# Splitting the expert weight loads in three, moving the fetch of the sorted rows to GpSimd, and reordering the quad loop of a routed feed-forward layer

## The reference

```
x = hidden_states.reshape(-1, h)
shared_out = _swiglu(x, shared_gate_w, shared_up_w, shared_down_w)
logits = x @ gate_w
topk_ids = jnp.argmax(logits, axis=-1)
topk_val = jnp.max(logits, axis=-1)
scores = jax.nn.sigmoid(topk_val)[:, None]
xs = x * scores
order = jnp.argsort(topk_ids)
sorted_x = xs[order]
g = _grouped_mm(sorted_x, routed_gate_w, tokens_per_expert)
u = _grouped_mm(sorted_x, routed_up_w, tokens_per_expert)
d = _grouped_mm(jax.nn.silu(g) * u, routed_down_w, tokens_per_expert)
routed_out = d[inv]
return (shared_out + routed_out).reshape(b, s, h)
```

## Time and profile before

| what | us |
|---|---|
| median of 3 runs (353.39 to 355.84) | 354.5 |
| the profiled execution's own time | 352.22 |
| its span | 350.4 |
| TensorE busy | 300.3 |
| VectorE busy | 206.3 |
| ScalarE busy | 134.8 |
| GpSimd busy | 56.0 |
| transfers issued by SyncE, share of 16 DMA engines | 47.9% |
| mean granted clock of TensorE | 0.951 |

### The profile page before, as it was taken

One profiled execution on the slowest core, in us unless ns is written; L12 is line 12 of the kernel. 1 busy time (PEld: TensorE's weight loads), 2 busy tenths in 40 slices (PEclk: granted clock), 3 DMA queues, 4 the chain that ended last, 5 costly groups with the idle time before them and its releaser, 6 DMA issues.

```text
span 350.4 us, 6874 instructions
## 1 busy us (share of the span) xinstructions
PE 300.3 (86%) x2484; PEld 213.8 (61%) x2484; DVE 206.3 (59%) x589; ACT 134.8 (38%) x309; POOL 56.0 (16%) x73
## 2 busy tenths in 40 slices
PE   1996979388899999999975999989899999964958
PEld 1774548277899999998963766665454555421322
DVE  0454684433465665665266699948739867645653
ACT  1021242243242242242233466529147545615650
POOL 0111000100110110110000001111711210442350
PEclk9999899879999999999997799999999999996996
DMA  7999991003364264053597200000389996899231
GB/s 291 397 435 426 410 316 48 2 0 111 131 241 151 91 239 147 34 181 129 233 353 285 85 2 2 6 4 0 86 299 395 394 354 251 336 358 397 49 46 17
DMA packets 13115, 67.73 MB, mean 193 GB/s; under 512 B 1738, under 2 KB 7322, under 8 KB 8986
## 3 DMA queue, kind: packets, MB, share of 16 engines
q1 hardware_dynamic: 11050, 64.28, 47.9%
q0 software_dynamic: 2032, 3.02, 4.1%
HBM read 61.38 MB, written 5.91 MB: 192 GB/s over the span
## 4 chain that ended last, share of the span: by engine, by line
PE 64%; issue 11%; DMA 10%; DVE 8%; ACT 3%; SPq 1%; DVEq 1%; POOL 1%; ACTq 0%
PE P L340 17%; PE P L460 8%; PE P L448 8%; PE P L628 7%; DMA arena<-experts_dram 7%; PE P L374 4%; PE P L484 4%; PE P L510 3%; PE P L436 2%; PE P L641 2%; DMA vrow<-sorted_x 2%; DMA arena<-patches_dram 2%; PE P L525 1%; DVE arena L996 1%; PE P L535 1%
## 5 line engine op out<-in xcount | busy, mean ns | idle before, releaser
L340 PE MATMUL P<-arena 128*104 128x256 f32 x288 | 73.5, 395 | 9.4 <-DMA arena<-patches_dram 7.1
L340 PEld LDWEIGHTS P<-arena 128*104 128x104 f32 x288 | 47.4, 176 | 22.4 <-issue 8.3
L1290 POOL TENSOR_TENSOR rstd<-var,mhalf 104x1 f32<-104x1 f32 x40 | 21.9, 548 | 210.5 <-DVE var L919 210.5
L628 PE MATMUL P<-arena,cols 128*32 128x512 f32 x288 | 37.3, 664 | 11.1 <-ACT cols L849 9.1
L824 ACT ACTIVATE arena<-arena 128x1024 f32 x31 | 31.5, 1051 | 21.2 <-SPq L325 9.1
L460 PE MATMUL P<-arena 128*128 128x104 f32 x256 | 29.9, 275 | 2.4 <-ACT arena L764 2.4
L460 PEld LDWEIGHTS P<-arena 128*128 128x128 f32 x256 | 29.7, 192 | 3.1 <-issue 1.4
L448 PEld LDWEIGHTS P<-arena 128*128 128x128 f32 x256 | 29.8, 192 | 1.2 <-issue 0.7
L448 PE MATMUL P<-arena 128*128 128x104 f32 x256 | 29.8, 275 | 0.5 <-issue 0.5
L628 PEld LDWEIGHTS P<-arena,cols 128*32 128x32 f32 x288 | 9.1, 120 | 32.6 <-issue 19.1
L764 ACT ACTIVATE arena<-P,arena 128x104 f32<-128x104 f32 x64 | 17.0, 348 | 27.7 <-PE P L448 27.7
(11 more groups left out here) (200 smaller groups left out, 480.3 us busy)
## 6 DMA issues: line engine op xcount, KB each, us to landing
arena<-experts_dram SPq DMA_DIRECT2D x22, 1536.0 KB, 8.4
arena<-experts_dram SPq DMA_DIRECT2D x8, 2048.0 KB, 12.7
arena<-patches_dram SPq DMA_DIRECT2D x4, 624.0 KB, 6.3
sorted_x<-arena SPq DMA_DIRECT2D x1, 2056.0 KB, 35.2
arena<-shared_dram SPq DMA_DIRECT2D x1, 1536.0 KB, 32.4
arena<-w_dram SPq DMA_DIRECT2D x1, 1024.0 KB, 9.8
out_dram<-arena SPq DMA_DIRECT2D x1, 1024.0 KB, 33.7
out_dram<-h POOLq DMA_DIRECT2D x8, 104.0 KB, 4.9
```

What stands on the lines that cost most here:

```text
L340: last = mm(P[b][0:a.shape[1], col:col + D], a, rhs(c), start=(c == 0), stop=(c == chunks - 1))
L628: last = mm(P[b][part, :], xT[:, c, part], weights(u)[:, c * INNER:(c + 1) * INNER], start=(c == 0), stop=(c == DC - 1), tile_position=(0, ...
L1290: nc.gpsimd.tensor_tensor(rstd[:, :], var[:, :], mhalf[:, :], ALU.pow).then_inc(s["rstd_ready"], 1)
```

## The change

- A weight load becomes three transfers of a third (gate, up, down) on the same semaphore; it counts as landed when all three have.
- GpSimd issues the three fetches of quads 0 to 6 right after its scatter; SyncE issues weights alone.
- `x3T` lies in the place of the queries, `zB` in that of the padded keys. The first copies wait for the scaled rows and no longer for `hid_ready`; `hidden(5)`, `(6)` and `(7)` come between and behind the copies of quad 0, and `hidden(3)` behind the first table.
- On TensorE the products that turn the tables round stand one `shared_up` piece earlier each. `shared_down(1)` moves ahead of quad 0; the others are spread as none, 2, 3, 4 and 5, 6 and 7 over quads 0 to 4 (before: 1; 2 and 3; 4 and 5; 6 and 7 over quads 0 to 3).
- `y_evac` writes into the rows of its own quad, so nothing waits for an earlier addition; target rows are computed for eight quads at once.
- In the loop the rows of the coming quad are fetched one turn ahead and transposed first, and ScalarE and VectorE copy gate and up weights before `hT_evac` and `y_evac`. Two fetches, of blocks 8 and 9, take the place of one, and `sorted_x` is one block longer.
- The register loads drop their bounds checks (one assertion is left where five or more stood).

```diff
-SORTED = (MAX_QUADS + 1) * 128
+BLOCKS = MAX_QUADS + 2
+SORTED = BLOCKS * 128
-YBUFS = 4
+SHARED_FIRST = 2
+SHARED_AT = ((), (2,), (3,), (4, 5), (6, 7), (), (), ())
-        oT = x3T = kz
+        oT = kz
+        x3T = qT
-        zB = flat5[:, 0:2 * HALF].rearrange("p (a n) -> p a n", a=2)
+        zB = quad[:, 0:2 * HALF].rearrange("p (a n) -> p a n", a=2)
             def feed(of, lane):
                 e, at, free = of
                 sp.wait_ge(s["copied_dve"], free)
                 sp.wait_ge(s["copied_act"], free)
-                sp.dma_start(feeds_s[:, bass.ds(at, SLOT)], experts1[bass.ds(e, 1)].rearrange("e p n -> (e p) n")).then_inc(lane_in[lane], 16)
+                for n in range(3):
+                    sp.dma_start(feeds_s[:, bass.ds(at + n * THIRD, THIRD)],
+                                 experts1[bass.ds(e, 1), :, n * THIRD:(n + 1) * THIRD].rearrange("e p n -> (e p) n")).then_inc(lane_in[lane], 16)
             feed(entry(0), 0)
             second = entry(1)
-            sp.wait_ge(xs_sent, 16 * GROUPS)
-            window(0)
             feed(second, 1)
-            for i in range(1, len(WINDOW_PARTS)):
-                window(i)
             with pe.Fori(0, more) as i:
+                pe.wait_ge(l_window_in, 16 * (i + 2))
+                xt(STILL).then_inc(s["l_xt_done"], 1)
                 pe.wait_ge(s["l_hT_ready"], i + 1)
 ...
                 down_strips(STILL % 2).then_inc(s["l_dn_done"], 1)
-                pe.wait_ge(l_window_in, 16 * (i + 2))
-                xt(STILL).then_inc(s["l_xt_done"], 1)
             with act.Fori(0, more) as i:
-                act.wait_ge(s["l_ht_done"], i + 1)
-                hT_evac().then_inc(s["l_hT_ready"], 1)
                 need, where = weights_of(act, i + (STILL + 1))
                 act.wait_ge(s["loaded"], need)
                 copy_third(where[2], 0, gate_of(2))
                 copy_third(where[3], 0, gate_of(3))
+                act.wait_ge(s["l_ht_done"], i + 1)
+                hT_evac().then_inc(s["l_hT_ready"], 1)
+                act.wait_ge(s["l_xt_done"], i + 2)
+                xT_evac().then_inc(s["l_xT_ready"], 1)
                 copy_third(where[2], 1, up_of(2)).then_inc(s["l_gatew_in"], 1)
             dve.wait_ge(s["table_ready"], 1)
             need, where = weights_of(dve, 0)
-            hidden(7)
-            dve.wait_ge(s["hid_ready"], 2 * IC)
             dve.wait_ge(s["loaded"], need)
+            dve.wait_ge(s["xs_scaled"], GROUPS)
             copy_gate(where).then_inc(s["gatew_in"], 1)
+            hidden(5)
             copy_up(where).then_inc(s["upw_in"], 1)
-            shared_rows(0)
+            hidden(6)
             copy_down(where, 0).then_inc(s["copied_dve"], 1)
             need, where = weights_of(dve, 1)
+            hidden(7)
             with dve.Fori(0, more) as i:
 ...
+                mul().then_inc(s["l_hw_ready"], 1)
+                dve.wait_ge(l_window_in, 16 * (i + 2))
                 ids = xw[:, STILL, D:XROW]
 ...
                 dve.wait_ge(s["l_aimed"], i + 1)
+                dve.wait_ge(s["l_added"], 16 * (i + 2))
             pool.wait_ge(xs_sent, 16 * GROUPS)
+            for i, q in enumerate(WINDOW_PARTS):
+                end = (WINDOW_PARTS + (STILL,))[i + 1]
+                pool.dma_start(xw[:, q:end, :], sorted_x[q * 128:end * 128, :].rearrange("(r p) c -> p r c", p=128)).then_inc(windows_in[i], 16)
+                if r == STILL - 1:
+                    pool.wait_ge(s["l_xt_done"], 1)
+                    window(STILL + 1)
             with pool.Fori(0, more) as i:
-                pool.wait_ge(s["l_aim_ready"], i + 1)
-                pool.wait_ge(s["l_xt_done"], i + 1)
                 pool.wait_ge(s["l_turn"], i + 1)
-                window(i + (STILL + 1))
                 pool.wait_ge(s["l_y_ready"], i + 2)
 ...
                 add_rows(STILL, s["l_added"])
+                pool.wait_ge(s["l_xt_done"], i + 2)
+                pool.wait_ge(s["l_aim_ready"], i + 1)
+                window(i + (STILL + 2))
```

More of the change, by code:

```diff
@@ L44 @@
 SPILLS = STILL + 1
-YBUFS = 4
+SHARED_FIRST = 2
+SHARED_AT = ((), (2,), (3,), (4, 5), (6, 7), (), (), ())
 ROUND = float(2 ** 23)
 XROW = D + 1
+IN_TABLE = "VectorE bounds each entry when it makes the table"
 BQ0, BK0, LNS, LNB, AB, BQ1, BK1, B2, B1 = 0, 2, 4, 6, 8, 10, 12, 14, 30
@@ L195, in tower @@
         l_window_in = sem("l_window_in")
-        added = [sem(f"added{r}") for r in range(STILL)]
+        added = sem("added")
         pat_in = [sem(f"pat_in{i}") for i in range(4)]
@@ L298, in entry @@
                 row = table[0:1, FEED * n:FEED * (n + 1)] if isinstance(n, int) else table[0:1, bass.ds(n * FEED, FEED)]
-                _, (e, at, free) = nc.values_load_multi_w_load_instructions(row, engines=[sp.engine], min_val=0, max_val=(SLOTS - 1) * SLOT)
-                e = nc.s_assert_within(e, 0, EXPERTS - 1, skip_runtime_bounds_check_because="the table clamps it to EXPERTS - 1")
-                return e, at, nc.s_assert_within(free, 1, MAX_QUADS + 1, skip_runtime_bounds_check_because="the table keeps it at 1 or above")
+                _, (e, at, free) = nc.values_load_multi_w_load_instructions(row, engines=[sp.engine], min_val=0, max_val=(SLOTS - 1) * SLOT,
+                                                                              skip_runtime_bounds_check_because=IN_TABLE)
+                e = nc.s_assert_within(e, 0, EXPERTS - 1, skip_runtime_bounds_check_because=IN_TABLE)
+                return e, at, nc.s_assert_within(free, 1, MAX_QUADS + 1)
             def feed(of, lane):
@@ L601, in _ @@
             last.then_inc(s["prefix_done"], 1)
-            for n in range(2, 5):
+            for n in range(2, 4):
                 shared_up(n)
@@ L608, in _ @@
             last.then_inc(s["feeds_done"], 1)
-            shared_up(5)
+            shared_up(4)
             pe.wait_ge(s["blocks_ready"], 1)
@@ L613, in _ @@
             mm(records[:, :, LANES], tcol[0:64, 1:2], ident[0:64, bass.ds(LANES - 1, 16, LANES)], start=True, stop=True).then_inc(s["table_done"], 1)
-            for n in range(6, 2 * IC):
+            for n in range(5, 2 * IC):
                 shared_up(n)
@@ L651, in shared_down @@
                 rows(6 + g % 2, lambda c: hidT[:, c, gcol(g)], lambda c: sdw[:, c, :], IC).then_inc(s["sd_done"], 1)
-            shared_down(0)
+            for g in range(SHARED_FIRST):
+                shared_down(g)
             pe.wait_ge(s["table_ready"], 1)
@@ L681, in _ @@
                     next_xt(q + 1)
-                if q == 0:
-                    shared_down(1)
-                elif q <= 3:
-                    shared_down(2 * q)
-                    shared_down(2 * q + 1)
+                for g in SHARED_AT[q]:
+                    shared_down(g)
                 if q >= 1:
@@ L1243, in _ @@
                     aim_static()
[L1244 to L1247 removed]
+                for g in SHARED_AT[q]:
+                    shared_rows(g)
                 if q >= 1:
                     dve.wait_ge(s["dn_done"], q)
[L1250 to L1252 removed]
+                    y_evac(xw[:, q - 1, 0:D]).then_inc(s["y_ready"], 1)
                 if q < STILL:
@@ L1260, in _ @@
             nc.vector.nop().then_inc(s["l_turn"], 1)
-            dve.wait_ge(added[STILL - YBUFS], 16)
             with dve.Fori(0, more) as i:
-                dve.wait_ge(s["l_added"], 16 * (i + 1))
-                dve.wait_ge(l_window_in, 16 * (i + 1))
+                need, where = weights_of(dve, i + (STILL + 1))
+                dve.wait_ge(s["loaded"], need)
+                copy_gate(where)
+                copy_up(where).then_inc(s["l_gatew_in"], 1)
+                dve.wait_ge(s["l_dn_done"], i + 1)
+                y_evac(y_last).then_inc(s["l_y_ready"], 1)
+                copy_down(where, STILL % 2).then_inc(s["copied_dve"], 1)
+                dve.wait_ge(s["l_sgate_ready"], i + 1)
+                dve.wait_ge(s["l_up_done"], i + 1)
+                mul().then_inc(s["l_hw_ready"], 1)
+                dve.wait_ge(l_window_in, 16 * (i + 2))
                 ids = xw[:, STILL, D:XROW]
@@ L1334, in _ @@
                 add_rows(STILL, s["l_added"])
-            for r in range(STILL):
-                pool.wait_ge(added[r], 16)
-            pool.wait_ge(l_window_in, 16 * (more + 1))
+                pool.wait_ge(s["l_xt_done"], i + 2)
+                pool.wait_ge(s["l_aim_ready"], i + 1)
+                window(i + (STILL + 2))
+            pool.wait_ge(added, 16 * STILL)
+            pool.wait_ge(l_window_in, 16 * (more + 2))
             pool.wait_ge(s["l_added"], 16 * (more + 1))
```

66 lines of the change are left out of this document (24 added, 42 removed).

## The result

The change makes the kernel slower: 362.14 us (356.02 to 366.25, 20 runs) against 354.71 us (352.06 to 356.12, 20 runs) for the kernel before on the same chip, +7.4 us in the medians. The ratio of undisturbed runs is 1.0123, 95% interval 1.0097 to 1.0150; that comparison leaves out runs over 1.5% above a kernel's fastest, and the changed kernel's own runs spread over 10 us, so its ratio lies under that of the medians, 1.021. The prediction was 355.1, in a range of 351.3 to 359.0: wrong.

A forecast was written before the change was run, and what follows sets the result against it. Bound: a chain of waits, the moment quad 4 is copied, five loads at full rate, then the end. Terms 0 - 1.4 + 0.8 + 1.2 = +0.6 us on 354.5 gave 355.1 us, range 351.3 to 359.0.

The forecast's parts named there:

- A: From the last shared_up piece's start to the tenth load's issue, which follows quad 4's copies; predicted -1.4 us.
- B: From the tenth load's issue to the last load's landing, the last five loads; predicted +0.8 us.
- the thirds: Weight loads split in three: shorter rows cost the last five loads 0 to 1.5 us; taken as +0.8.
- C: From the last load's landing to the end of quad 7's ht; the prediction had no term for it.
- the end: From the end of quad 7's ht to the span's end: later eviction, a last fetch behind the product; +1.2 us.
- its own signs: Wrong if five loads took under 23 or over 28 us, quad 4 was copied before 298 or after 302, or clock stayed full.
- the barrier behind the last landing: At the program's end, a barrier after a later landing; 0.2 us within the +1.2.
- quad 4: Copied earlier because TensorE's pieces are spread differently, so the load of 301.44 is issued at 300.0; -1.4 us.
- Earlier start of the loads: 0: First two loads begin some 3.3 us earlier, but later loads wait for slots; worth 0, at most 3.3 us.
- My rival for GpSimd's fetches: GpSimd's five fetches go out late beside VectorE's copies of quad 0, quad 1 slips 3 us: 358.1 us; chance 0.07.
- each third pays a start of its own: Each added transfer of the last five loads costs 0.5 us, thirds cost 5.0: 359.3 us; chance 0.15.
- Stage D: From the end of quad 7's ht to the span's end, 15.4 us before; predicted +1.2 us.

The follow-up runs named there:

- e6: The changed kernel with the three fetches of quads 0 to 6 back on SyncE and the second load behind the scatter; +7.1 us, ratio 1.012 to the kernel before.
- e11: e8 with ScalarE's gate and up copies again ahead of the last quad's eviction; +0.5 us, ratio 0.999 to the kernel before.
- e15: e8 repeated unchanged on another occasion; -0.3 us, ratio 0.989 to the kernel before.
- e16: e8 with VectorE's y_evac moved ahead of the up weights' copies in the loop; -0.6 us, ratio 0.994 to the kernel before.
- e1: The changed kernel run again as a control; +8.9 us, ratio 1.022 to the kernel before.
- e8: e4 plus the three fetches on SyncE and the second load behind the scatter; 350.9 us, -3.1 us, ratio 0.990 to the kernel before.
- e4: The changed kernel with whole loads, the last fetch early and hT_evac ahead of the loop's copies; 357.9 us, +3.1 us, ratio 1.008 to the kernel before.
- e14: The kernel before with only the weight loads split into thirds; +2.4 us, ratio 1.006 to the kernel before.
- e9: e8 with the weight loads in thirds again; +1.2 us, ratio 0.999 to the kernel before.
- e2: The changed kernel with the loop's last fetch released ahead of the blank quad's product; +5.8 us, ratio 1.013 to the kernel before.
- e10: e8 with the last fetch again waiting for target rows behind the blank quad's product; -0.6 us, ratio 0.998 to the kernel before.
- e5: The kernel before, unchanged, one profile as a control; no timing given, 43.3 us from the last shared_up piece's start to the tenth load's issue.
- e12: The kernel before with only the three fetches moved to GpSimd, second load not waiting for the scatter; +0.2 us, ratio 0.998 to the kernel before.
- e13: e4 with GpSimd still fetching but the second load held until the scatter has landed; +2.6 us, ratio 1.010 to the kernel before.
- e7: The changed kernel with GpSimd still fetching but the second load held until the scatter has landed; +8.6 us, ratio 1.025 to the kernel before.

## Why the prediction was wrong

The sum gave +0.6 us, the profiled executions +7.4. By stages, measured less predicted: A -1.1 (-2.5 against -1.4), B +3.1 (+3.9 against the thirds' +0.8), C +1.7 (not in the sum), the end +3.1 (+4.3 against +1.2). By its own signs, too, it was wrong: the last five loads took 29 us, over its 28. The steps that failed are the thirds, stage C, and the barrier behind the last landing; the head start cost something in other executions.

- **What bounds the kernel, and quad 4: right, a little too careful.** Quads 0, 1 and 3 start at 265.1, 270.9 and 287.2, predicted 266.0, 271.7 and 287.9; the tenth load is issued at 299.0, not 300.0. Stage A is 2.5 us shorter, the term was -1.4. It is 41.0 in e6 to e11, e15 and e16, where the second load no longer starts ahead of the scatter, against 43.3 to 43.9 in the kernel before: the reordering is worth about 2.5.
- **"Earlier start of the loads: 0": a term put at nothing without a row.** I let the head start dissolve in the wait for slots, and did not ask what else uses the DMA engines between the first load and quad 0. It is the scatter and the fetch. In the profiled execution that hid (the scatter lands after 5.3 us, quad 0 is still early); in e1 quad 0 is 8.9 us behind the last piece and partly at the 1.2 GHz level (5.34 us instead of 3.64), and stage A 3.0 longer. e8 against e4 shows the size with whole loads, 6 us; in the change itself, with thirds, it is 1.8 by the medians (e6). A reading was wrong beside it: the scatter did not release the fetch at 257.03. It was down by 255.96, when GpSimd issued its own fetch, and SyncE was still in its register loads. My rival for GpSimd's fetches had the right place and the wrong mechanism: GpSimd's issues were not slow (0.6 to 0.9 us each), the transfers were.
- **Thirds, +0.8: the term that was too small.** Measured 2 to 3 us by the ratio (e14 +2.0, e9 +3.2); stage B is 3.9 longer in the profiled execution. The price of a short row fits two stretches of three; I applied it to the last five loads alone. The earlier loads are slower as well, and while the engines are full what they leave over (0.57 MB, 1.7 us at 329 GB/s) is moved in stage B. Another 0.39 MB (1.2 us) is GpSimd's, and half of that is the later stores and not the thirds. The last five loads have ten more issues, not six; that changed nothing in the sum. The 2.0 us that the prediction takes from the Trainium skill ("DMA: Bandwidth & Descriptors", Anatomy of one DMA) is given there for transfers issued by GpSimd, and these are SyncE's. The rival "each third pays a start of its own" named a time near the result (359.3), but nothing here needs starts that don't overlap: the share stays at 0.94 to 1.02.
- **Stage C, +1.7: a term that was missing.** I read the clock at the end of the program only. A late landing leaves TensorE idle before quads 6 and 7 too, and quad 7's products then take 5.3 us. The five profiles with a C of 9.6 or more (the change, e1, e2, e6, e11) are those with a B of 27.8 or more.
- **The end, +1.2: right up to the last wait, in part by luck.** `hT_evac` at +3.03 behind `ht` (+3.1 predicted), down at +3.8 (+3.8), the fetch landed at +16.6 (+16.4). But I had the full clock in down and half in the blank quad's products, from +5.7 to +12.2. It was half in down and came back within the products, which ran from +7.2 to +12.1: two errors that cancel. The step that failed is "a term of +1.0, and 0.2 for the barrier": 15.4 before was counted to the span's end with GpSimd's drain hidden under TensorE, 16.4 to a landing on GpSimd with that drain still to come, 3.1 us. By the ratios, e2 and e10 put the late fetch at 3 us, and e11 the late eviction at 3 more. (Stage D of the kernel before is 12.5 in e5, where the clock stays up, and 15.4 in the first profile.)

## What to carry to other kernels

When an edit makes large loads start earlier, list the small transfers that share the DMA engines with them and stand on the critical path: the order in which one engine issued them is gone once another engine issues some, and a small fetch just behind a 1.5 MB load waits for nearly all of it. Count an end to the last engine's closing instruction, and give each engine its own (here 2.3 to 2.6 us on GpSimd, 0.45 on TensorE). Where engines are full, an earlier issue with more bytes left over is no gain: compare bytes moved, not issue times.

## What the runs showed that I had not expected

- The same fetch of 128 rows takes 2.0 us (3.4 at most, in e15) where the load ahead of it is through and the next comes behind it (e6, e8 to e11, e15, e16). It takes 5.7 us just behind a load on that load's own queue (the kernel before) and 6.3 and 7.1 on GpSimd's (e12, e13).
- Parts of a change that look separate are not: moving the fetch costs 0.2 us on the kernel before (e12) and 6 us in e4 (against e8, on another chip).
- The run's time goes with TensorE's granted clock. Beside e13 to e16 the kernel before took 349.8 to 352.9 us in the runs with a mean clock of 0.951 or more, and 352.9 to 355.7 in those at 0.942. The changed kernel has more stalls after which the clock falls, and its runs spread over 10 us instead of 4.
- Open: why stage B is 29 us in the change, e1 and e2 but 26.4 to 27.9 with thirds in e6, e7, e9 and e14; and why e11 and e15 have 27 to 28 with whole loads, where the other nine have 24.6 to 25.5 (e11's profile is its slowest run).
